# Attention denominators of a landmark-attention and mixture kernel: computed once per head, inverted on 128x128 values, copied out to the channels by DMA

## The reference, cut to what matters

```python
out_unnorm = einsum('bhnk,bhkd->bhnd', Phi_Q, Y)          # numerators: 16 channels per head
norm = einsum('bhnk,bhko->bhno', Phi_Q, solve(W_kernel, Phi_K_sum))
norm = maximum(norm, 1e-10)                               # denominator: one per token and head
out = out_unnorm / norm
x = layernorm(x + out @ Wo.T + bo)
x = layernorm(x + moe(x))                                 # 8 experts, top 2, all computed
```

## Time and profile before

| | us |
|---|---|
| median of 3 executions | 2036.72 (2035.22 to 2041.76) |
| the profiled execution | 2037.47 |
| its span, first to last instruction | 2035.7 |
| PE busy in the span | 1791.6 (88%) |
| DVE busy | 1541.5 (76%) |
| ACT busy | 1220.1 (60%) |
| POOL busy | 932.0 (46%) |

### The profile page before, as it was taken

The page is one execution under the profiler, slowest core; times in us unless marked ns, Lnnn a source line. Parts: engine busy times, 40 slices in busy tenths (PEclk is TensorE's granted clock), DMA queues, the critical chain, the costliest instruction groups (busy, mean ns, idle before and its releaser), DMA issues.

```text
span 2035.7 us, 43517 instructions
## 1 busy us (share of the span) xinstructions
PE 1791.6 (88%) x16696; PEld 1331.2 (65%) x16696; DVE 1541.5 (76%) x3285; ACT 1220.1 (60%) x2427; POOL 932.0 (46%) x1179
## 2 busy tenths in 40 slices
PE   4578989989985898999999999989999899998997
PEld 3267878877772566676666666666666667666665
DVE  5668844898434787888888788888888888888874
ACT  2246666766655466558657566755765656675554
POOL 2300000000001375667675667666666666766666
PEclk8689999999996899999999999999999999999999
DMA  2586797777965233433343333334333333334300
GB/s 86 89 168 150 160 185 151 175 170 159 192 154 134 68 91 78 93 93 89 73 109 84 88 90 77 89 88 104 84 78 91 92 96 77 94 79 98 89 27 22
DMA packets 210864, 214.30 MB, mean 105 GB/s; under 512 B 59232, under 2 KB 142560, under 8 KB 210400
## 3 DMA queue, kind: packets, MB, share of 16 engines
q1 hardware_dynamic: 210464, 210.99, 44.7%
q0 software_dynamic: 192, 0.52, 0.1%
HBM read 61.50 MB, written 23.59 MB: 42 GB/s over the span
## 4 chain that ended last, share of the span: by engine, by line
PE 41%; DVE 26%; POOL 12%; issue 11%; SPq 5%; DMA 3%; ACT 2%; DVEq 0%; POOLq 0%; ACTq 0%
PE bank L300 9%; PE bank L302 8%; PE bank L301 8%; POOL x_tok L550 3%; PE bank L1600 3%; PE bank L1628 2%; PE bank L1490 2%; DMA q_stack<-key_aug 2%; POOL part_x L563 2%; POOL part_x L562 2%; PE bank L1506 2%; DVE nrm L1194 2%; PE bank L1491 2%; DVE phi L1020 2%; DVE inversion L1048 2%
## 5 line engine op out<-in xcount | busy, mean ns | idle before, releaser
L300 PE MATMUL bank<-weh,x1h 128*128 128x512 f32 x1024 | 439.2, 429 | 75.3 <-DVE y_out L1293 39.6
L302 PE MATMUL bank<-wel,x1h 128*128 128x512 f32 x1024 | 418.2, 408 | 0.0
L301 PE MATMUL bank<-weh,x1l 128*128 128x512 f32 x1024 | 417.8, 408 | 0.0
L300 PEld LDWEIGHTS bank<-weh,x1h 128*128 128x128 f32 x1024 | 201.4, 197 | 195.5 <-issue 65.2
L550 POOL TENSOR_TENSOR x_tok<-x_tok,bo_sb 128x1024 f32<-128x1024 f32 x32 | 77.7, 2427 | 533.7 <-DMA x_tok<-in_x 533.7
L838 ACT ACTIVATE part_x<-bank,gate 128x256 f32<-128x256 f32 x512 | 211.8, 480 | 164.9 <-PE bank L302 164.6
L776 ACT ACTIVATE phi<-bank,nlt,invt 128x512 f32<-128x512 f32 x256 | 186.9, 792 | 83.0 <-PE bank L1600 83.0
L302 PEld LDWEIGHTS bank<-wel,x1h 128*128 128x128 f32 x1024 | 199.9, 195 | 48.5
L642 ACT ACTIVATE phi<-bank,invt 128x512 f32<-128x512 f32 x256 | 162.6, 684 | 104.6 <-PE bank L1491 104.5
L301 PEld LDWEIGHTS bank<-weh,x1l 128*128 128x128 f32 x1024 | 200.2, 196 | 36.2
L562 POOL TENSOR_TENSOR part_x<-part_x 128x512 f32<-128x512 f32 x128 | 180.4, 1409 | 28.9 <-ACT part L838 28.8
(11 more groups left out here) (199 smaller groups left out, 4319.7 us busy)
## 6 DMA issues: line engine op xcount, KB each, us to landing
x_raw<-in_xT SPq DMA_DIRECT2D x64, 512.0 KB, 4.4
q_stack<-kh SPq DMA_DIRECT2D x256, 128.0 KB, 2.4
x_tok<-in_x SPq DMA_DIRECT2D x32, 512.0 KB, 4.0
q_stack<-kl SPq DMA_DIRECT2D x128, 128.0 KB, 2.4
q_stack<-key_aug SPq DMA_DIRECT2D x128, 128.0 KB, 2.6
k_hl<-attn_h SPq DMA_DIRECT2D x32, 256.0 KB
k_ha<-attn_h SPq DMA_DIRECT2D x32, 256.0 KB
k_hl<-attn_l SPq DMA_DIRECT2D x32, 256.0 KB
```

The source lines that it names most:

```text
L300: nc.tensor.matmul(outp, ah, bh, start=first, stop=False)
L301: nc.tensor.matmul(outp, al, bh, start=False, stop=False)
L302: return nc.tensor.matmul(outp, ah, bl, start=False, stop=last)
```

## The change

The denominators are computed once per head: `denominators(q)` runs 32 small matmuls (8 pairs of heads by 4 token tiles), which accumulate over the pairs. `y_cur` now has only one nonzero column per head there, so that the 16 heads of token tile t stand in rows 32t to 32t + 15 of 128 columns of bank 5. `invert_denominators(q)` clamps and inverts these 128x128 values into `den_inv`. `spread_inverses(q)` on SP copies every head's row to its 16 channels in `attn` by eight DMAs. `normalise(q, s)` multiplies the numerators of bank 4 + s by that, in place. `attention` is left with the numerators. `denominators(q)` stands on PE between `experts` 7 and 8 and needs all eight pairs of `phi`; on DVE `invert_denominators(q)` stands behind the clamp of the pairs 6 and 7, `normalise(q, 0)` behind `x1_lo`, `finish(p, 1)` is moved ahead of `queries_lo(q+1)`, and `normalise(q, 1)` stands where `norm_begin(q, 1)` was. The logits' transpose follows `attention(q, 1)`. The first two chunks are changed in the same manner.

```diff
+            def spread_inverses(c):
+                if past_end(c):
+                    return
+                sp.wait_ge(inv_ready, c + 1)
+                sp.wait_ge(attnl_ready, 2 * c)
+                for s in range(KC):
+                    for t in range(TPC):
+                        heads = slice(32 * t + HPS * s, 32 * t + HPS * s + HPS)
+                        sp.dma_start(attn[:, s, t * P:(t + 1) * P],
+                                     rep(den_inv[heads, :], 1, HD)).then_inc(inv_spread, 16)
...
                         sp.dma_start(x_tok[:], x_v[bass.ds(p + 2, 1)].rearrange("a p t d -> (a p) t d")).then_inc(xt_loaded, 16)
+                    spread_inverses(p + 2)
                     stack_queries(p + 3)
...
-            def norm_begin(c, s, at=4):
...
-            def norm_end(c, s, at=4):
...
+            def invert_denominators(c):
+                if past_end(c):
+                    return
+                dve.wait_ge(den_done, c + 1)
+                dve.wait_ge(inv_spread, SPREAD * c)
+                V.tensor_scalar(den_inv[:], bank[5][:, 0:P], NORM_MIN, None, ALU.max).then_inc(den_read, 1)
+                dve.wait_ge(den_read, c + 1)
+                V.reciprocal(den_inv[:], den_inv[:]).then_inc(inv_ready, 1)
+            def normalise(c, s):
+                if past_end(c):
+                    return
                 dve.wait_ge(out_done, 2 * c + s + 1)
+                dve.wait_ge(inv_spread, SPREAD * (c + 1))
+                V.tensor_tensor(attn[:, s], bank[4 + s][:], attn[:, s], ALU.mult).then_inc(attn_ready, 1)
...
                     q_clamp(q, range(2, 4))
                     q_clamp(q, range(4, 6))
-                    norm_begin(q, 0)
                     finish(p, 0)
                     q_clamp(q, range(6, 8))
+                    invert_denominators(q)
                     combine(p, 2, me)
-                    norm_end(q, 0)
                     x1_lo(c, nxt)
+                    normalise(q, 0)
+                    finish(p, 1)
                     queries_lo(q + 1)
-                    finish(p, 1)
                     gates_begin(c)
-                    norm_begin(q, 1)
+                    normalise(q, 1)
                     combine(p, 3, me)
                     gates_end(c, nxt)
                     query_norms(q + 1)
-                    norm_end(q, 1)
                     first_tile(c, nxt)
...
+            def denominators(c):
+                if past_end(c):
+                    return
+                pe.wait_ge(qphi_ready, PAIRS * (c + 1))
+                pe.wait_ge(attn_ready, 2 * c)
+                for i in range(PAIRS):
+                    for t in range(TPC):
+                        last = mm(bank[5][32 * t:32 * t + 32, 0:P], y_cur[:, i, 32:64], phi[:, i, t * P:(t + 1) * P],
+                                  start=(i == 0), stop=(i == PAIRS - 1))
+                last.then_inc(den_done, 1)
...
                     attention(q, 0)
                     experts(p, 7, me)
+                    denominators(q)
                     experts(p, 8, me)
...
-                    attention(q, 1, logits=c)
-                    if past_end(q):
-                        logit_transpose(c)
+                    attention(q, 1)
+                    logit_transpose(c)
```

More of the change, by code:

```diff
@@ L294, in program @@
         STACKED = 16 * 16
+        SPREAD = 16 * KC * TPC
         KH_STACKED, AUG_STACKED = 16 * 6, 16 * TPC
@@ L459, in _ @@
             stack_queries(1)
+            spread_inverses(0)
             sp.wait_ge(xql_ready, 3)
@@ L463, in _ @@
             sp.dma_start(x_tok[:], x_v[1]).then_inc(xt_loaded, 16)
+            spread_inverses(1)
             stack_queries(2)
@@ L1183, in landmark_values @@
                     V.tensor_tensor(y_cur[half, :, 16 * u:16 * u + 16], y[half, :, 0:HD], y_bias[half], ALU.add)
-                    last = V.tensor_copy(y_cur[half, :, 32 + 16 * u:48 + 16 * u],
-                                         y[half, :, HD:HD + 1].broadcast_to([64, PAIRS, HD]))
+                    own_columns = y_cur[half].rearrange("p i c -> p (i c)")[:, 32 + u:33 + u + 66 * (PAIRS - 1):66]
+                    last = V.tensor_copy(own_columns, y[half, :, HD])
                 last.then_inc(y_ready, 1)
-            def norm_begin(c, s, at=4):
+            def invert_denominators(c):
[7 more added lines that the diff above has]
+            def normalise(c, s):
                 if past_end(c):
@@ L1192, in norm_begin @@
                 dve.wait_ge(out_done, 2 * c + s + 1)
-                dve.wait_ge(attn_ready, 2 * c + s)
-                own.then(V.tensor_scalar(nrm[:], bank[at + 1][:], NORM_MIN, None, ALU.max))
-                own.did(V.reciprocal(nrm[:, 0:CH // 2], nrm[:, 0:CH // 2]))
-            def norm_end(c, s, at=4):
[L1199 to L1204, removed]
+                dve.wait_ge(inv_spread, SPREAD * (c + 1))
+                V.tensor_tensor(attn[:, s], bank[4 + s][:], attn[:, s], ALU.mult).then_inc(attn_ready, 1)
             def residual_stats(c, at):
@@ L1318, in _ @@
             query_norms(1)
[L1319 to L1322, removed]
+            invert_denominators(0)
+            normalise(0, 0)
+            normalise(0, 1)
             dve.wait_ge(winv_stored, 32)
@@ L1331, in _ @@
             q_clamp(1, range(4, 8))
-            norm_begin(1, 0)
+            invert_denominators(1)
             x1_lo(0, 0)
-            norm_end(1, 0)
+            normalise(1, 0)
+            queries_lo(2)
             gates_begin(0)
-            queries_lo(2)
+            normalise(1, 1)
             gates_end(0, 0)
             query_norms(2)
-            norm_begin(1, 1)
-            norm_end(1, 1)
             def first_tile(p, at, first=False):
@@ L1617, in landmark_solve, with attention @@
                 last.then_inc(y_done, 1)
-            def attention(c, half, at=4, logits=None):
+            def denominators(c):
[8 more added lines that the diff above has]
+                last.then_inc(den_done, 1)
+            def attention(c, half):
                 if past_end(c):
@@ L1623, in attention @@
                 pe.wait_ge(qphi_ready, PAIRS * c + 4 * half + 4)
[L1624 to L1631, removed]
+                pe.wait_ge(attn_ready, 2 * c)
+                if half:
+                    pe.wait_ge(den_read, c + 1)
+                for j in range(4):
+                    last = mm(bank[4 + half][32 * j:32 * j + 32, :], y_cur[:, 4 * half + j, 0:32], phi[:, 4 * half + j],
+                              start=True, stop=True)
                 last.then_inc(out_done, 1)
@@ L1723, in _ @@
             pe.wait_ge(y_ready, 1)
+            denominators(0)
             attention(0, 0)
-            attention(0, 1, 2)
+            attention(0, 1)
             query_dists(1, range(PAIRS))
             output_projection(0)
+            denominators(1)
             attention(1, 0)
@@ L1731, in _ @@
             gate_logits(0, 0)
-            attention(1, 1, logits=0)
+            attention(1, 1)
+            logit_transpose(0)
             query_norms(2)
```

6 lines of the change are left out of this document (3 added, 3 removed).

## The result

The changed kernel takes 2319.68 us, median of four runs (2319.41 to 2320.26), against 2035.97 (2030.54 to 2041.76) of the kernel before beside it: ratio 1.1393, 95% interval 1.1362 to 1.1425. The prediction of slower was right. Its 2142 us, and its range up to 2190, were far too low.

A forecast was written before the change was run, and what follows sets the result against it. PE was held fullest, with a regular 2.5 us gap behind DVE. A 7.0 us clamp end plus a 19.1 us chain delayed step 14; with clock, 3.5 us over 30 turns gave 2142 us, range 2085 to 2190.

The forecast's parts named there:

- the term of the eight transfers: SP's DMAs spreading the inverses, between inversion and `normalise(q, 0)`: 6.9 us, or 5.3 at the shortest issue.
- The rest of the chain: Steps from the clamp through denominators, inversion, transfers and DVE work to expert step 14: 19.1 us in all, transfers included.
- The clock: PE's granted clock falls behind gaps: net +0.4 us per turn, range -0.9 to +1.4; falling every turn was a 0.12 rival.
- DVE's work: Fewer clamps and reciprocals on DVE: about 7.2 us less per turn, some 220 us less busy time.
- "In time": Query splitting for `query_norms(q+1)` and ACT's `attn_hi(q, 0)`, queued behind `normalise(q, 0)`, come before PE needs them at steps 12 and 13.
- The first two chunks: Before the repeating turns, saved reciprocals offset one inversion and the transfers: 0 us, bounds -4 and +4.
- The mechanism of the stall: PE waits at `denominators` for the clamp of pairs 6 and 7, delayed by `finish(p, 0)` and POOL: 4.6 us per turn.
- The other side, faster: Rival, chance 0.07: the gap at step 14 closes and no stall opens; 2004 us, or 1962 with short transfers.
- the 75 of the whole gap: PE's gap before expert step 14, behind DVE's `combine`: at most some 2.5 us per turn to win, 75 us over 30.
- PE waits for DVE nowhere else regularly: DVE's shorter work, about 7.2 us per turn, pays only through PE's gap before expert step 14.

The follow-up runs named there:

- The fastest version: Changed kernel with multiplications behind `query_norms`, last clamp ahead of `finish(p, 0)`, doubled rows, denominators behind expert 8 and x1 transposes: 1994.64 us, 0.9802 of the kernel before.

## Why the prediction was wrong

**The step that failed is the term of the eight transfers**: 6.9 us, with 5.3 and 6.9 as bounds, where 12.04 were measured. From the wait's end to step 14 the turn shown has 1321.60 - 1296.04 = 25.6 us, where I had 19.1: 5.1 of the 6.5 are this term, 1.5 the denominators at the lower clock. I took the pace from the nearest rows, whose transfers read 32 partitions, and took issue plus one landing as the whole; source partitions didn't enter. The versions with 16 and 32 of them confirm the term for what it described (6.77 us). The upper bound should have been open: no row of before showed a transfer with this form of the source. The Trainium skill's rule on the number of engines, above, was the one to weigh against 8 source rows, and I did not.

**The rest of the chain held.** Beside the predicted steps: the clamp that PE waits for releases it 1296.04 - 1289.05 = 7.0 us after `attention(q, 0)` (predicted 7.0), the wait is 4.33 (4.6), inversion 1.3 (1.3), `finish` 1.1 (1.1), `queries_lo` 1.4 (1.4), `gates_begin` from 1315.90 to 1319.95, 4.05 (4.1), multiplication and `combine` together 1.65 (1.66). With 12.0 in place of 6.9 the predicted turn of 45.9 becomes 51.0, and the mean is 51.7. With 32 source partitions the turn is 46.7.

**The clock** was a smaller miss. I set +0.4 us per turn net. In this kernel the denominators behind the wait took more than 1.95 us in 24 of the 31 chunks in view, 3.0 on average: +1.0 us. The mean granted clock between 760 and 1960 is 0.91, against 0.97 before.

**DVE's work** fell by 173 us, and I had said some 220. Line 1316 accounts for 41 of the missing 47: it is busy 125.6 us in the span, where the same line of the kernel before was busy 84.2. An instruction of DVE that is held up by POOL counts as busy. DVE's idle time before `normalise(q, 0)` is 9.28 us in the turn shown, not 4 to 5, which is the failed term again.

**"In time" was not in time.** I held that the queries' split, queued behind `normalise(q, 0)`, would come in time for `query_norms`. PE waits there 3.44 us in the turn shown. It adds nothing to the sum by itself, because the same chain releases step 14 a little later, and it goes when the transfers are short: with 32 source partitions this wait is not in the list between 760 and 1960 at all.

**The first two chunks** were set at 0, bounds -4 and +4, and cost 16.8 us. There nothing lies beside the transfers: DVE stands idle 16.99 us before `normalise(0, 0)`, and PE 10.06 before the distances behind it. The versions with single rows reach their first gate transpose between 697.7 and 704.7, those with doubled rows between 686.7 and 695.9; so a good part of it is the transfers again, and the spread within each kind stays unexplained.

**The mechanism of the stall** held, with one addition. POOL's `split_lo` meets `finish` and the clamp as the earlier trace rows suggested: line 1316 takes 2.55 us, and the one that starts behind `split_lo` is held up until that ends. This is `finish` in the changed kernel (2.55 us) and with the clamp ahead of it (2.60 us: there the clamp gets in before `split_lo`, which takes 2.83 us instead of 2.34), and the clamp in the version with late multiplications and the clamp ahead (2.78 us). `split_lo` in the three, in this order:

```profile
1291.84 2.34 POOL L553 TENSOR_TENSOR xl<-x_raw,xh 128x1024 fp32r<-128x1024 f32 x1
```

```profile
1310.49 2.83 POOL L553 TENSOR_TENSOR xl<-x_raw,xh 128x1024 fp32r<-128x1024 f32 x1
```

```profile
1278.71 2.36 POOL L553 TENSOR_TENSOR xl<-x_raw,xh 128x1024 fp32r<-128x1024 f32 x1
```

The Trainium skill's rule that the later one blocks fully (SBUF — State Buffer, "Who interferes with whom") fits all three. What I had not seen is that the order of the two still matters, since PE waits directly for the clamp: 80 us in two pairs of runs (2319.7 to 2239.3, 2134.1 to 2053.8), 43 in a third, with the denominators later (2037.4 to 1994.6).

**The rivals.** The other side, faster, needed the clamp at PE's arrival and short transfers. The fastest version gets there from both sides: it has the clamp ahead of `finish(p, 0)`, without which it is 43 us slower, it lets PE arrive later, and of the waits for transfers only 16.0 us for `q_stack` are left. Even so it wins 42 us: more than the 29 of the run without reciprocals, whose order was that of the kernel before, and not the 75 of the whole gap. Behind the gap at step 14 stood other waits of PE, which my "PE waits for DVE nowhere else regularly" left out.

## What to carry to other kernels

A transfer inside the SBUF is priced by its source form too: before taking a duration from a neighbouring row, compare how many partitions both read, and if it is 8 where the row has 32, leave the upper bound open. A result that goes through DMAs should be asked for as late as its reader allows, and everything queued behind the asking instruction, and behind the DMAs on their own queue, belongs to their price. Relief on an engine with a gap in front of it is worth less than the gap, because the next waits stand right behind it.

## What the runs showed of the hardware

- Eight transfers that read 8 partitions of 512 bytes, each 16 times, and write 128 partitions needed 10.0 us for their data, 52 GB/s. With 16 source partitions and the same bytes the rate was 97 GB/s, with 32 it was 98. The median issue on SP is 0.82 us with 8 source partitions and 0.60 with 16 or 32, so slower transfers hold the issuer back; the longest issues don't show it, since they are 1.49 us with 8 and 1.80 with 32. With 16 or 32 a transfer lands in 2.5 or 2.2 us.
- Doubling rows in the matrix that PE multiplies by made a 128-row result with every value twice, at 1.95 us for the 64 instructions as without it, and so gave the transfers their 16 source partitions at no time on PE.
- Behind long waits of PE the denominators ran at the lower clock: in the changed kernel every group behind a wait of 3.5 us or more took 2.57 to 3.64 us, for work that takes 1.95 at full clock. In the turn shown the granted clock is 1.00 from 1290 to 1294 and 0.54 from 1296 to 1299.5. In the fastest version, without the wait, 31 of 32 groups take 1.95 or 1.96.
- An instruction of DVE that starts while POOL's `split_lo` runs lasts until that ends, 2.55 us instead of 0.41 for line 1316, and the profile counts the wait as busy.
